# An order of its own for each kind of slot on four engines of a Mamba-2 and feed-forward kernel

## What is computed

```python
# block 1: Mamba-2 layer, 32 heads of 64, state size 64, 8 groups, causal conv of 4 taps
proj = rmsnorm(layernorm(x)) * norm_w @ in_proj_w      # z 2048 | x 2048 | B 512 | C 512 | dt 32
xBC  = silu(depthwise_conv4(proj[xBC]) + conv_b)
dt   = softplus(proj[dt] + dt_bias);  dA = exp(-dt * exp(A_log))
h_t  = dA_t * h_{t-1} + (dt_t * x_t) B_t^T;   y_t = h_t C_t + D * x_t
g    = y * silu(z);  g = g * rsqrt(mean over each of 8 groups(g^2) + eps) * gate_norm_w
x    = x + g @ out_proj_w
# block 2: layernorm -> layernorm -> ternary w1 -> exact gelu -> layernorm -> ternary w2, added to x
```

## Time and profile before

| | |
|---|---|
| three runs | 1258.92, 1261.83, 1263.74 us; median 1261.83 |
| profiled execution | 1256.21 us, span of the core 1254.4 us, mean granted TensorE clock 0.981 |
| busy over the span | PE 1083.5 us (86%), weight loads 722.7 us, DVE 1120.6 us (89%), ACT 975.4 us (78%), POOL 888.6 us (71%) |
| DMA | 24.94 MB, mean 20 GB/s |

### The profile page before, as it was taken

One profiled execution on the slowest core, in us unless ns is written; L12 is line 12 of the kernel. 1 busy time (PEld: TensorE's weight loads), 2 busy tenths in 40 slices (PEclk: granted clock), 3 DMA queues, 4 the chain that ended last, 5 costly groups with the idle time before them and its releaser, 6 DMA issues.

```text
span 1254.4 us, 26469 instructions
## 1 busy us (share of the span) xinstructions
PE 1083.5 (86%) x8970; PEld 722.7 (58%) x8970; DVE 1120.6 (89%) x1967; ACT 975.4 (78%) x2798; POOL 888.6 (71%) x600
## 2 busy tenths in 40 slices
PE   0624788999999999999999999999999999987786
PEld 0613456666666666666666666666666666653565
DVE  7788899999999999999999999999999999867985
ACT  2556788888888888888888888888888888843353
POOL 7460267877787888788878887888788877894331
PEclk9997899999999999999999999999999999997999
DMA  5500000000000000000000000000000000101201
GB/s 154 186 0 0 9 2 1 2 2 2 26 2 2 2 27 2 2 1 26 2 2 2 26 2 2 2 26 2 2 2 18 1 2 2 35 29 37 98 26 34
DMA packets 28756, 24.94 MB, mean 20 GB/s; under 512 B 12112, under 2 KB 22992, under 8 KB 28368
## 3 DMA queue, kind: packets, MB, share of 16 engines
q1 hardware_dynamic: 24400, 21.18, 5.5%
q10 hardware_dynamic: 4224, 2.10, 0.5%
HBM read 14.88 MB, written 8.39 MB: 19 GB/s over the span
## 4 chain that ended last, share of the span: by engine, by line
PE 55%; DVE 25%; issue 8%; ACT 7%; POOL 4%; DMA 1%; ACTq 0%; POOLq 0%; DVEq 0%; SPq 0%
DVE conv L1077 9%; PE bank L1441 7%; PE bank L1458 7%; DVE lm L1066 6%; PE bank L1464 5%; PE bank L1385 5%; PE bank L1401 4%; PE bank L1387 4%; PE bank L1386 4%; PE bank L1417 3%; PE bank L1432 3%; PE bank L1496 3%; PE bank L1473 2%; POOL w_lo L584 2%; DVE cdec L1107 2%
## 5 line engine op out<-in xcount | busy, mean ns | idle before, releaser
L1077 DVE SCALAR_TENSOR_TENSOR conv<-bank,cw,conv 128x511 f32<-128x511 f32 (+2 forms) x576 | 410.7, 742 | 24.3 <-ACT conv L768 21.8
L1066 DVE TENSOR_TENSOR_SCAN lm<-bank,ident 128x512 f32<-128x512 f32 x256 | 298.7, 1209 | 49.2 <-PE bank L1401 49.2
L615 POOL TENSOR_TENSOR lm<-lm,cbs 128x1024 f32<-128x1024 f32 x128 | 303.4, 2370 | 51.2 <-ACT xw L760 49.8
L798 ACT ACTIVATE xdt<-bank,dt_all 128x64 f32<-128x64 f32 x1024 | 222.5, 332 | 0.0
L601 POOL TENSOR_TENSOR gated<-gated,gate 128x512 f32<-128x512 f32 x128 | 164.4, 1284 | 74.1 <-DVE gated L1116 72.2
L760 ACT ACTIVATE xw<-xdt,lm 128x64 f32<-128x64 f32 x768 | 196.3, 339 | 0.0
L621 POOL TENSOR_TENSOR ssum<-ssum,sq 128x512 f32<-128x512 f32 x96 | 123.2, 1284 | 83.6 <-ACT sq L812 82.8
L1385 PE MATMUL bank<-xn_hi,w_hi 128*128 128x512 f32 x320 | 151.4, 473 | 26.2 <-DVE conv L1077 25.5
L607 POOL TENSOR_TENSOR gated<-gated,rbs 128x512 f32<-128x512 f32 x128 | 165.1, 1290 | 1.3 <-ACT rbs L861 1.3
L1458 PEld LDWEIGHTS bank<-lm,xdt 128*64 128x64 f32 x2048 | 109.2, 136 | 78.8 <-issue 78.1
L1441 PE MATMUL bank<-gated,w_out 128*128 128x512 f32 x256 | 148.9, 665 | 3.2 <-POOL gated L607 3.1
(11 more groups left out here) (183 smaller groups left out, 1801.6 us busy)
## 6 DMA issues: line engine op xcount, KB each, us to landing
lm<-in_L_attn_in_proj_w SPq DMA_DIRECT2D x1, 2048.0 KB, 9.9
xn_scratch<-chan SPq DMA_DIRECT2D x4, 512.0 KB, 4.8
r_stage<-residual_scratch SPq DMA_DIRECT2D x8, 256.0 KB, 3.0
x_scratch<-r_stage SPq DMA_DIRECT2D x8, 256.0 KB, 2.0
cbs<-x_scratch SPq DMA_DIRECT2D x8, 256.0 KB, 2.8
gated<-x_scratch SPq DMA_DIRECT2D x1, 2048.0 KB, 7.9
out_tokens<-gated ACTq DMA_DIRECT2D x8, 256.0 KB, 2.3
xn_stage<-xn_scratch SPq DMA_DIRECT2D x7, 256.0 KB, 3.2
```

The source lines that it names most:

```text
L615: gp.tensor_tensor(lm[:, mr, :, :], lm[:, mr, :, :], cbs[:, :, :], ALU.mult).then_inc(m_done, 1)
L798: act.activation(xdt[:, r, at:at + HP], misc_of("xt", n)[:, at:at + HP], ACT.Copy, scale=dt_h).then_inc(xdt_done, 1)
L1066: V.tensor_tensor_scan(lm[:, m % R, a, :], bc_bank[(3 * m + a) % 2][:, :], ident4[:, :], 0.0, ALU.mult, ALU.add).then_inc(scanned, 1)
L1077: V.scalar_tensor_tensor(out=conv[:, ci % 4, shift:S], in0=tile_bank(b, n, t)[:, 0:S - shift], scalar=cw[:, q, t, KW - 1 - shift:KW - shif ...
```

## The change

The arithmetic stays the same. The turn of each engine is cut into small functions, and each kind of slot calls them in an order of its own. On PE the y product becomes two pieces, so that rows can stand between them, and each piece keeps only the waits that it needs: y within chunks for the decay product and the skip term before it, y from states for the state steps and the decayed C. The taps get an order of their own for each kind (`TAPS`), tile 1 goes ahead of tile 0, and the order in which small products take the two banks (`MISC`) follows the new order of PE. The functions are those of before but for their names.

```diff
-PLAN = [[2], [3, 4], [0, 1], [5]]
+PLAN = [[2], [3, 4], [1, 0], [5]]
+TAPS = [[(2, 1), (2, 2), (2, 3)], [(3, 1), (3, 2), (4, 1), (3, 3), (4, 2), (4, 3)],
+        [(1, 1), (0, 1), (1, 2), (1, 3), (0, 2), (0, 3)], [(5, 1), (5, 2), (5, 3)]]
...
@@ misc_plan: order of the small products in the two banks
-            plan.append((n, "xt", LAG_SSD, 0))
-            plan.append((n, "s", LAG_STATE, 0))
             if r == 0:
                 plan.append((n, "var", LAG_VAR, 0))
+            if r < 2:
+                plan += [(n, "s", LAG_STATE, 0), (n, "xt", LAG_SSD, 0)]
+            else:
+                plan += [(n, "xt", LAG_SSD, 0), (n, "s", LAG_STATE, 0)]
...
@@ POOL, one turn (before: gate, normalise, decay product, square sum, root)
+                gate_product()
+                if r == 0:
+                    decay_product(); normalise(); root()
+                elif r == 3:
+                    normalise(); square_sum(); decay_product()
+                else:
+                    normalise(); decay_product(); square_sum()
...
@@ ACT, one turn
+                if r == 0:
+                    weigh(); convolve(); activate(0); copy_variance()
+                    scale_x(); square(); gate_silu(); copy_cb()
+                elif r == 1:
+                    convolve(); weigh(); activate(0); expand_root()
+                    scale_x(); square(); gate_silu(); copy_bt(); copy_factor()
+                elif r == 2:
+                    convolve(); weigh(); scale_x(); activate(0)
+                    square(); copy_output(); activate(1); gate_silu()
+                else:
+                    weigh(); convolve(); activate(0); activate(1)
+                    scale_x(); square(); gate_silu(); next_high()
...
@@ DVE, one turn, after the two scans; taps(a, b) are taps a to b-1 of TAPS[r]; skip() ends each
+                if r == 0:
+                    taps(0, 1); state_step(0); taps(1, 2); state_step(1)
+                    taps(2, 3); state_step(2); chunk_ends()
+                elif r == 1:
+                    taps(0, 1); state_step(0); taps(1, 2); state_step(1)
+                    taps(2, 3); state_step(2); taps(3, 5); chunk_ends(); taps(5, 6)
+                elif r == 2:
+                    taps(0, 2); state_step(0); taps(2, 3); state_step(1)
+                    taps(3, 4); chunk_ends(); taps(4, 5); state_step(2); taps(5, 6)
+                else:
+                    state_step(0); taps(0, 1); chunk_ends(); taps(1, 2)
+                    state_step(1); taps(2, 3); state_step(2)
...
@@ PE, one turn; "ahead" is the slot after this one
+                if r == 0:
+                    out_product(); tiles(); variance(); states(); gate_tile(); transposes()
+                    y_within(); rows(ssd, 2); rows(ahead, 0); y_states(); cb_products()
+                elif r == 1:
+                    tiles(); states(); transposes(); out_product()
+                    y_within(); rows(ssd, 2); rows(ahead, 0); y_states()
+                    gate_tile(); b_transposes(); factor_transposes()
+                elif r == 2:
+                    tiles(); transposes(); states(); out_product()
+                    y_within(); rows(ssd, 2); y_states(); gate_tile(); rows(ahead, 0)
+                else:
+                    transposes(); states(); tiles(); gate_tile(); y_within()
+                    rows(ssd, 2); out_product(); rows(ahead, 0); y_states()
+                    next_input(); last_output()
+                rows(ahead, 1)
```

More of the change, by code:

```diff
@@ L55, in tap_numbers @@
         for r in range(R):
[L56 to L59, removed]
+            for t, shift in TAPS[r]:
+                found[q, t, shift] = n
+                n += 1
     return found
@@ L1407, in slot, with transposes @@
                 ssd = back(b, n, LAG_SSD)
+                ahead = back(b, n + 1, LAG_SSD)
+                yy = back(b, n, LAG_Y)
                 if isinstance(b, int) and (b, n) == (0, R):
                     pe.wait_ge(tap, NTAP // UNITS)
-                if ssd is not None:
+                def transposes():
+                    if ssd is None:
+                        return
                     bb, m = ssd
@@ L1418, in slot, with tiles, states @@
                     last.then_inc(xt_ready, 1)
-                if real:
-                    for t in PLAN[r]:
-                        project(b, n, t, (b, n))
-                st = back(b, n, LAG_STATE)
-                if st is not None:
+                def tiles():
+                    if real:
+                        for t in PLAN[r]:
+                            project(b, n, t, (b, n))
+                def states():
+                    st = back(b, n, LAG_STATE)
+                    if st is None:
+                        return
                     bb, m = st
@@ L1465, in slot, with variance @@
                     last.then_inc(y_ready, 1)
-                if r == 0 and back(b, n, LAG_VAR) is not None:
+                def variance():
+                    if back(b, n, LAG_VAR) is None:
+                        return
                     bb, m = back(b, n, LAG_VAR)
@@ L1519, in slot @@
                     last.then_inc(xo_ready, 1)
-                if back(b, n + 1, LAG_SSD) is not None:
-                    for k in range(2):
-                        spread(*back(b, n + 1, LAG_SSD), k)
+                if r == 0:
+                    out_product()
+                    tiles()
+                    variance()
+                    states()
+                    gate_tile()
+                    transposes()
+                    y_within()
+                    rows(ssd, 2)
+                    rows(ahead, 0)
+                    y_states()
+                    cb_products()
+                elif r == 1:
+                    tiles()
+                    states()
+                    transposes()
+                    out_product()
+                    y_within()
+                    rows(ssd, 2)
+                    rows(ahead, 0)
+                    y_states()
+                    gate_tile()
+                    b_transposes()
+                    factor_transposes()
+                elif r == 2:
+                    tiles()
+                    transposes()
+                    states()
+                    out_product()
+                    y_within()
+                    rows(ssd, 2)
+                    y_states()
+                    gate_tile()
+                    rows(ahead, 0)
+                else:
+                    transposes()
+                    states()
+                    tiles()
+                    gate_tile()
+                    y_within()
+                    rows(ssd, 2)
+                    out_product()
+                    rows(ahead, 0)
+                    y_states()
+                    next_input()
+                    last_output()
+                rows(ahead, 1)
             def step(i, par, k):
```

276 lines of the change are left out of this document (195 added, 81 removed).

## The result

The changed kernel takes 1189.97 us (median of 4 runs, 1186.81 to 1192.76), the kernel before 1260.38 (1257.03 to 1263.74): the ratio is 0.9441, 95% interval 0.9403 to 0.9478, so 5.6% less time. I forecast 1224 us, with 1209 to 1249 as the range. In the rounds of experiments three executions of the kernel before (1394, 1755 and 5346 us) and one of the run with the output product and z tile moved (5517 us) were disturbed and are left out of all medians and ratios.

What follows compares the result with a forecast made beforehand. Bound: PE and DVE's lock-step hand-over at each slot's end. Unit 30.83 falls to 29.6 (PE 29.5 plus 0.1), times 31 saves 38.1; drain adds 0.8: 1218.9 profiled, plus 5.6 to the median, 1224 us, range 1209 to 1249.

Steps and rivals of the forecast that it cites:

- What bounds the kernel: PE and DVE at each slot's end: a hand-over in lock-step, no full engine; larger turns sum to 30.7 against 30.83.
- PE alone: 29.5, bounds 29.2 and 29.9: PE's work in us for one unit of four slots under the new order, without pauses.
- three tails of 0.1: PE's busy 29.59 a unit: modelled tails before three waits, some 0.1 each, vanish when the wait does.
- my 0.1 for missed slacks: Added to PE's 29.5 a unit, for slacks under 0.5 that some units will miss.
- PE has more room than its busy time says: Rival: PE's pieces shrink when nothing paces them, DVE's 28.66 a unit is the floor; 1196 us, chance 0.03.
- DVE keeps up: DVE over a unit: 28.66 of work plus about 1.0 of waits, full at 29.7 at most.
- The splitting of y: PE's y product in two parts: costs only the switch, gives DVE its chunk ends 0.8 earlier.
- Switches: PE going between kinds of product: about 0.1 each; row groups 8 to 9, tile groups 8 to 7, neutral.
- The tightest wait: PE's variances in kind 0, waiting for POOL's square sum of kind 3: slack 0.5.
- The slower loop through the C B copies: Rival: ACT and POOL loop, some 28.3 us, becomes the bound; unit 31.3 gives 1276 us, chance 0.09.
- The lock stays: Rival: row 1 still closes PE's turn, DVE's lead unchanged, unit stays 30.8; 1262 us, chance 0.05.
- three signs of being wrong: PE waits for the square sum before variances, C B copies wait for POOL, or PE's pieces grow between y's parts.

Runs made afterwards that it cites:

- the replay: Kernel of PE's products of a unit alone, no waits, no other engine, in four orders: 28.59 us a unit in the order before, 28.60 in the change's.
- the fourth order: PE's order of the change with the states put next to y within, played on PE alone without waits: 27.4 us a unit, three units in 82.3.
- the kernel of pairs: Kernel of matmuls alone: each kind of PE product twelve times by itself, then pairs in turn; y within and output product take 2.08 us, alone 0.87 each.

## Why the prediction was right or wrong

**What bounds the kernel: right in the main.** PE and DVE did walk in lock-step, and in the changed kernel both are full. But I told the lock as one of two engines. ACT's first tap lies on it as well: undoing ACT's order costs 48 us, more than undoing DVE's.

**The step that failed** is one term of the sum: "PE alone: 29.5, bounds 29.2 and 29.9". PE's work measured 28.59 in the order before and 28.60 in the new one, 0.9 less than the term and outside its bounds. I took it from the busy column, 29.59. By the terms beside it, three tails of 0.1 and a neutral sum, it should have read 29.3 and not 29.5, which is still 0.7 too much. The busy column stands too high because a matmul's modelled end lies behind the moment at which the next could start, so that a short wait hides in it: in the replay a row is 0.38 long and the next piece starts 0.31 later, and four transposes are 0.66 long and the next piece starts 0.41 later. Kinds 3, 0 and 1 lost 0.14, 0.39 and 0.50 to waits while their timeline showed none but 0.23. I read PE as needing 8.1 in kind 1; it needed 7.57 and waited there too.

**The sum.** With the replayed 28.60 in place of 29.5 and my 0.1 for missed slacks it would read 30.83 - 28.70 = 2.13, times 31 is 66.0, less 0.8 for the drain: 1256.2 - 65.2 = 1191.0 for the profiled execution, which took 1192.8. So the mechanism was right and this term was mis-sized. That sum is partly lucky: the mean unit was 31.01 before and 28.83 after, both longer than the ones read in detail. The lower bound has a slip of its own: a unit of 29.2 gives 1261.8 - 50.5 + 0.8 = 1212 us, and not the 1209 that I wrote, since the drain makes the time longer.

**The rival that came nearest in time** was "PE has more room than its busy time says", 1196 us, to which I gave 0.03. My argument against it was that kind 3 ran without a wait for 6.22 us, so that the distance is the cost; alone it takes 6.08, so 0.14 of waiting was in that distance. But its mechanism was not the one that I wrote: the pieces don't shrink when nothing paces them, and the floor is PE's 28.6, with DVE's 28.27 right under it. The Trainium skill says in "Perfetto Trace Analysis", section "Identifying the Most-Contended Engine", that matmul busy time isn't the measure of how near TensorE is to its limit. The runs agree with that: 29.59 busy stood for 28.59 of work. They don't bear out the share of weight loads that it names instead: this is 70% (19.84 of 28.54) in the changed kernel, in which PE runs within 0.06 us of its own length.

**DVE keeps up: right.** Its lag in kind 3 is 0.97 (638.21 against 637.24; I had 0.9 to 1.0). Its lead is 0.35 at the end of kind 0, where I had 0.6, and none at the end of kind 1 (658.75 against 658.73), where I had half a microsecond. It waits 0.26 a unit rather than 1.0, and its work is 28.27, 0.39 less than before, where I had counted on 0.2. Of its order I wrote that the early decayed C frees PE in kind 2; DVE's order alone gives 22 us of the 31 that I then expected, and undoing it costs 34.

**The splitting of y: overrated.** I called "rows 0 and 1 are PE's last work" the first cause of the lock. With row 0 last again and y whole the time is 1193 us, within the interval of the change, so this cause isn't borne out with the other orders new. With POOL's order as before, the same edit costs 0.7% (0.9512 against 0.9447), so the split is worth something there. Nor is it likely that a saving of PE's work hides its loss: in the replay the split makes the three pieces 0.01 longer, though that very order was not replayed.

**Switches: neutral, as written, but for another reason.** I priced a switch at about 0.1 and counted groups of rows and tiles. What costs is going to and from products whose weights fill only 64 columns or rows. By a count of visits in which the two parts of y are one, the change has three more (12 for 9), 0.8 to 1.1 us; the replay has 28.60 against 28.59. The count that fits takes the two parts of y (weights of 128 by 64 and of 64 by 64) as two even when they touch, since together they take no less than parted; only groups of the same weights join, as in the fourth order, where states next to y within save 1.2 us for four. This reading is mine, from these rows; it was not tested by pairs of its own.

**The tightest wait, ACT's and POOL's waits: right** in place and nearly in size, slack 0.26 for 0.5, ACT's waits 1.16 and 0.69 for 1.1 and 0.6. That POOL's new order matters shows only together with the split of y: undone alone it changes nothing, undone with it the time is 0.7% longer. The slower loop through the C B copies didn't bind (slack 0.6: the decay product ends at 650.51, the copies start at 651.14). "The lock stays" is excluded. None of the three signs of being wrong appeared: all of them watched for a slower unit, and none for a lower floor of PE.

**What stays open.** Why PE's order in the old surroundings costs 3.3%, and the rest of the change without PE's order 1.8%, is told by waits on their traces, not tested part by part. ACT's order alone and POOL's alone were not run.

## What to carry to other kernels

When several engines run hand-written orders in lock-step, lay one period out on each and look for what closes the ring. The gain is a property of the set of orders: PE's order, worth 94 us in the set, was a loss of 3.3% alone. Before taking a floor from PE's busy column, play its instructions by themselves without waits: here one small kernel gave that floor to 0.1 us, and would have brought the forecast within a few microseconds. A piece that another engine waits for, with half a microsecond of slack, should be moved with care whatever its own length: moving the output product, 0.86 us a slot, ahead of the tiles was the larger part of a loss of 74 us.

## What the runs showed of the hardware

- PE's busy time hid 1.0 us of waiting in each 30.8: 29.59 busy for 28.59 of work.
- An output product (float32, 128 columns of weights) takes 0.86 us between groups whose weights also have 128 columns and 96 or 128 rows, 0.96 with a group of 64-column weights on one side, and 1.05 between two of them. A visit to such groups costs 0.25 to 0.37 in all (0.25 with the variances, 0.26 with a bfloat16 row, 0.30 with transposes, 0.34 with the output product, 0.37 with a tile).
- The C B products, with weights of 64 rows and 128 columns, cost a visit too: 0.35 with transposes, 0.30 with a row. Among the other groups of 128 columns (transposes, tiles, output product, rows) a switch costs 0.03 at most.
- In the kernel of pairs the granted clock fell to 0.50, so to 1.2 of 2.4 GHz, first while the variances' 2-column products ran alone (0.89 a group, then 1.71) and again among their pairs with y within, which took 1.9 instead of 1.03. It was back at full among pairs of y within and transposes.
